# A four-layer attention kernel: the second up half of the gated layer moves to another PSUM bank, and the top-ten layer selects its rows in column strips

## The reference

```python
# layer 1
scores = einsum('bnd,d->bn', base_hidden, score_w[0]) + score_b[0]
_, topk_idx = top_k(scores, 10)
sparse_hidden = take_along_axis(base_hidden, topk_idx[:, :, None], axis=1)
...
return base_hidden.at[arange(B)[:, None], topk_idx].set(attn_out)
# layer 2, end
x = silu(x @ Wgate) * (x @ Wup) @ Wdown
return residual + x
```

## Time and profile before

| | |
|---|---|
| runs | 1354.81, 1357.92, 1359.65 us (median 1357.92) |
| the profiled execution | 1358.02 us, its span 1356.2 us |
| mean granted TensorE clock | 0.943 of full |
| busy: TensorE, VectorE, ScalarE, GpSimd | 90%, 54%, 45%, 32% |
| instructions | 36206 |
| top-ten layer | about 655 to 785 us of the span |
| grouped layer | about 785 to 1210 us, 16 slots and an end |

### The profile page before, as it was taken

The page is one execution under the profiler, slowest core; times in us unless marked ns, Lnnn a source line. Parts: engine busy times, 40 slices in busy tenths (PEclk is TensorE's granted clock), DMA queues, the critical chain, the costliest instruction groups (busy, mean ns, idle before and its releaser), DMA issues.

```text
span 1356.2 us, 36206 instructions
## 1 busy us (share of the span) xinstructions
PE 1219.7 (90%) x14778; PEld 1028.2 (76%) x14778; DVE 728.2 (54%) x1656; ACT 610.4 (45%) x1464; POOL 428.3 (32%) x545
## 2 busy tenths in 40 slices
PE   4899999977899999999778869999999999998986
PEld 2566666655599999999567759889889888876665
DVE  5688787667322000000466457657656657636776
ACT  2455555422444544545222235445445445535542
POOL 3224446153323222226200134424424423332200
PEclk9999999876899999999866879999999999999998
DMA  9000000000489999999510010100100100000000
GB/s 313 2 2 2 2 2 18 9 17 25 136 287 327 338 354 361 352 354 314 179 52 2 2 41 22 40 22 21 41 22 21 41 22 21 21 2 1 18 17 33
DMA packets 91572, 130.73 MB, mean 96 GB/s; under 512 B 13392, under 2 KB 74064, under 8 KB 91280
## 3 DMA queue, kind: packets, MB, share of 16 engines
q1 hardware_dynamic: 85360, 117.11, 26.0%
q0 software_dynamic: 4768, 10.26, 2.1%
q10 hardware_dynamic: 1280, 1.04, 0.2%
HBM read 116.82 MB, written 11.57 MB: 95 GB/s over the span
## 4 chain that ended last, share of the span: by engine, by line
PE 76%; DVE 11%; issue 4%; ACT 3%; DMA 3%; POOL 2%; SPq 1%; another core or an unknown queue 1%; ACTq 0%; DVEq 0%; POOLq 0%
PE scores L1776 9%; PE bank L1786 9%; PE scores L1470 8%; PE bank L2326 8%; PE bank L491 5%; PE bank L1470 4%; PE scores L508 4%; DVE reg L880 3%; PE scores L518 3%; PE bank L540 3%; PE scores L2316 3%; PE scores L2302 3%; PE bank L500 3%; PE bank L529 2%; PE scores L1978 2%
## 5 line engine op out<-in xcount | busy, mean ns | idle before, releaser
L1821 ACT ACTIVATE w_ca<-scores,fc1b 128x128 f32<-128x128 f32 x312 | 114.1, 367 | 139.3 <-PE scores L1776 117.2
L1776 PEld LDWEIGHTS scores<-reg 128*128 128x128 f32 x1248 | 145.2, 192 | 7.0 <-issue 2.5
L1776 PE MATMUL scores<-reg 128*128 128x128 f32 x1248 | 146.3, 275 | 3.8 <-DMA reg<-in_fc 1.2
L880 DVE TENSOR_REDUCE reg<-scores 128x8 f32<-128x1024 f32 x96 | 113.0, 1220 | 64.2 <-PE scores L508 55.6
L2396 ACT ACTIVATE reg<-reg,mx 128x128 f32<-128x128 f32 x256 | 99.3, 389 | 106.8 <-DVE mx L2547 106.8
L1855 DVE TENSOR_TENSOR reg<-bank,reg 128x256 f32<-128x256 f32 x39 | 16.6, 425 | 240.9 <-PE bank L1786 225.5
L1786 PE MATMUL bank<-reg,w_ca 128*128 128x256 f32 x624 | 141.1, 379 | 0.3 <-DVE small L1846 0.3
L1786 PEld LDWEIGHTS bank<-reg,w_ca 128*128 128x128 f32 x624 | 115.6, 190 | 14.5 <-DVE small L1846 0.3
L1470 PEld LDWEIGHTS scores<-reg 128*128 128x128 f32 x1024 | 116.8, 192 | 1.9 <-ACT reg L2404 1.1
L1470 PE MATMUL scores<-reg 128*128 128x128 f32 x1024 | 117.0, 275 | 0.5 <-ACT reg L2404 0.5
L2326 PE MATMUL bank<-reg,w_ca 128*128 128x256 f32 x496 | 115.1, 385 | 0.0
(11 more groups left out here) (305 smaller groups left out, 2375.2 us busy)
## 6 DMA issues: line engine op xcount, KB each, us to landing
reg<-in_fc SPq DMA_DIRECT2D x78, 1024.0 KB
w_sa<-grouped_values SPq DMA_DIRECT2D x64, 128.0 KB, 2.6
reg<-expert_out SPq DMA_DIRECT2D x16, 256.0 KB, 3.5
xres<-in_x SPq DMA_DIRECT2D x4, 512.0 KB, 11.4
ctxr<-in_ctx SPq DMA_DIRECT2D x1, 2048.0 KB, 15.3
w_l<-in_w_l SPq DMA_DIRECT2D x2, 1024.0 KB, 13.0
routed_rows<-reg SPq DMA_DIRECT2D x8, 256.0 KB
grouped_values<-reg SPq DMA_DIRECT2D x16, 128.0 KB, 1.7
```

What stands on the lines that cost most here:

```text
L880: ins = nc.vector.tensor_reduce(mxpad.rearrange("p (c n d) -> p n c d", c=C, d=DH)[:, 4 * half:4 * half + 4, :, 0], scores4[:, 2 * half:2 ...
L1776: ins = nc.tensor.matmul(S[n % 4][:, 0:P], up_w8[j % 2][:, c, f * P:(f + 1) * P], xbT[:, j % 2, c, :], start=(c == 0), stop=(c == C - 1))
L1821: nc.scalar.activation(h1[:, j % 2, f, :], S[n % 4][:, 0:P], ACT.Gelu, bias=fc1b[:, bass.ds(e * FC + f, 1)]).then_inc(M["fc1_free"], 1)
```

## The change

**Grouped layer.** The job u1 gets home "c" (bank 7, where the second query half qb lives) in slots t < B - 1, that is for batches 0 to 13. In slots 15 and 16 it stays in bank 0. The order of instructions is the same on every engine.

**Top-ten layer.** `chosen_rows` takes the selector of a batch (128 x 32) as the stationary side and the batch's 256 columns of xres as the moving side, and writes to the 32 partitions of the bank that belong to the batch: job "xr". The rows come out unturned. ScalarE copies them, with the turned selector, to chosen_T. A new TensorE step, `turn_chosen`, turns the two 128x128 halves into a new job "xg", and a new ScalarE step, `turned_copy`, writes them over the unturned ones. For groups 1 to 3 `turn_chosen` stands behind the value products of the group before, ahead of the queries; `turned_copy` stands ahead of `even_heads`. For group 0 both follow at once.

```diff
--- before.py
+++ after.py
@@
         tok_turned = junk[:, 0:4, :].rearrange("p k n -> p (k n)")
 
         KV = ["hc0", "hc1", "k0", "k1", "v0", "v1"]
-        in_turn = [("bias", 0)] + [(n, 2) for n in KV] + [("row", 0), ("xg", 0), ("q", 0)]
+        in_turn = [("bias", 0)] + [(n, 2) for n in KV] + [("row", 0), ("xr", 0), ("xg", 0), ("q", 0)]
         for g in range(G):
             if g + 1 < G:
-                in_turn += [("row", g + 1), ("xg", g + 1)]
+                in_turn += [("row", g + 1), ("xr", g + 1)]
             in_turn += {1: [("hc0", 3), ("hc1", 3)], 2: [("v0", 3), ("v1", 3)]}.get(g, [])
             if g + 1 < G:
-                in_turn += [("q", g + 1)]
+                in_turn += [("xg", g + 1), ("q", g + 1)]
             in_turn += {1: [("k0", 3), ("k1", 3)]}.get(g, [])
             if g + 1 == G:
                 in_turn += [("at", 0), ("at", 1), ("qa", 0), ("qb", 0), ("kv", 0)]
@@
         IN_TOP_TEN = [("at", 0), ("at", 1), ("qa", 0), ("qb", 0), ("kv", 0)]
         for t in range(-2, B + 1):
             for name, ahead, home in SLOT_JOBS:
+                if name == "u1" and t < B - 1:
+                    home = "c"
                 if 0 <= t + ahead < B and (name, t + ahead) not in IN_TOP_TEN:
                     job_at[name, t + ahead] = (home, n_jobs[home])
                     n_jobs[home] += 1
@@
                 ins.then_inc(tok_done(("row", g)), 1)
 
             def chosen_rows(g):
+                bank = tok_claim(pe, ("xr", g))
+                pe.wait_ge(M["tok_gat_ok"], g + 1)
+                for j in range(GB):
+                    nc.tensor.matmul(bank[mine(j), 0:D], gat[:, j, :], xres[:, g * GB + j, :], start=True, stop=True)
+                nc.tensor.transpose(bank[:, D:D + P], gat[:, :, :].rearrange("p j r -> p (j r)"), ident[:])\
+                    .then_inc(tok_done(("xr", g)), 1)
+
+            def turn_chosen(g):
                 bank = tok_claim(pe, ("xg", g))
-                pe.wait_ge(M["tok_gat_ok"], g + 1)
+                tok_await_moved(pe, ("xr", g))
                 for c in range(C):
-                    for j in range(GB):
-                        nc.tensor.matmul(bank[:, c * P + j * R:c * P + (j + 1) * R], xres[:, g * GB + j, c * P:(c + 1) * P],
-                                         gat[:, j, :], start=True, stop=True)
-                nc.tensor.transpose(bank[:, C * P:C * P + P], gat[:, :, :].rearrange("p j r -> p (j r)"), ident[:])\
-                    .then_inc(tok_done(("xg", g)), 1)
+                    ins = nc.tensor.transpose(bank[:, c * P:(c + 1) * P], chosen_T[:, g % 2, c * P:(c + 1) * P], ident[:])
+                ins.then_inc(tok_done(("xg", g)), 1)
 
             def queries(g):
                 bank = tok_claim(pe, ("q", g))
@@
             values(1, 2)
             score_rows(0)
             chosen_rows(0)
+            turn_chosen(0)
             queries(0)
             scores(0)
             for g in range(G):
@@
                 if g + 1 == G:
                     l2_keys_values(pe, 0)
                 if g + 1 < G:
+                    turn_chosen(g + 1)
                     queries(g + 1)
                 if g == 1:
                     keys(0, 3)
@@
                     .then_inc(tok_moved((f"v{v}", g)), 1)
 
             def chosen_copy(g):
-                bank = tok_await(act, ("xg", g))
+                bank = tok_await(act, ("xr", g))
                 if g >= 2:
                     act.wait_ge(M["tok_put_full"], g - 1)
-                nc.scalar.activation(chosen_T[:, g % 2, :], bank[:, 0:3 * P], ACT.Copy).then_inc(tok_moved(("xg", g)), 1)
+                nc.scalar.activation(chosen_T[:, g % 2, :], bank[:, 0:3 * P], ACT.Copy).then_inc(tok_moved(("xr", g)), 1)
+
+            def turned_copy(g):
+                bank = tok_await(act, ("xg", g))
+                nc.scalar.activation(chosen_T[:, g % 2, 0:D], bank[:, 0:D], ACT.Copy).then_inc(tok_moved(("xg", g)), 1)
 
             def queries(g):
                 bank = tok_await(act, ("q", g))
@@
             values(0, 2)
             values(1, 2)
             chosen_copy(0)
+            turned_copy(0)
             queries(0)
             for g in range(G):
                 if g + 1 == G:
@@
                 if g == 2:
                     values(0, 3)
                     values(1, 3)
+                if g + 1 < G:
+                    turned_copy(g + 1)
                 even_heads(g)
                 if g + 1 < G:
                     queries(g + 1)
@@
                 dve.sem_inc(tok_moved(("row", g)), 1)
                 link(nc.vector.tensor_tensor(place[:, own], n_above[:, own], n_tied[:, own], ALU.add))
                 if g > 0:
-                    tok_await(dve, ("xg", g - 1))
+                    tok_await(dve, ("xr", g - 1))
                 for j in range(GB):
                     ins = nc.vector.tensor_scalar(gat[:, j, :], ranks, place[:, g * GB + j:g * GB + j + 1], None, ALU.is_equal)
                 ins.then_inc(M["tok_gat_ok"], 1)
```

## The result

| | before | changed |
|---|---|---|
| runs | 1354.81 to 1362.88 us, median 1358.42 (5) | 1328.60 to 1342.55 us, median 1339.60 (5) |
| the profiled execution | 1358.02, span 1356.2 | 1328.60, span 1326.8 |
| instructions | 36206 | 36166 |

The ratio is 0.9853, with a 95% interval of 0.981 to 0.9896: 14 to 26 us less, 20 at the middle. Predicted were 18.9 us and 1339.

What follows compares the result with a forecast made beforehand. The chain of waits, three quarters of it TensorE, was taken to bound the kernel. -14.0 (grouped layer) - 4.9 (top-ten layer) = -18.9 us, from 1358.0 to 1339 us; own range 1334 to 1344, for 8 in 10 1333 to 1348.

Steps and rivals of the forecast that it cites:

- Edit 1: Grouped layer: second up half to bank 7 removes 14 holes ahead of the value products; -14.0 us, bounds 11.6 to 14.4.
- The selection: Top-ten layer: eight selector instructions in four overlapping strips take 1.1 us instead of 3.6, 2.5 us off each.
- The end "no overlap": Top-ten selection, other end of the estimate: strips run serially, 8 x 0.46 = 3.65 us, no gain at all.
- rival 1: Top-ten selections: strips don't overlap and stay at 3.65 us; -10.6 us in all, 1347 us; chance 0.07.
- The turns, group by group: Top-ten layer: turning chosen rows between value products and queries costs 1.2 us at half clock, 0.9 at full.
- Edit 2: Top-ten layer: selection in strips, then turning the chosen rows; -4.9 us together, bounds -5 - 5 and +3.4.
- Rival 2: Top-ten layer, group 3: TensorE loses its full clock, +11 us, so -8 in all, 1350 us; chance 0.06.
- Rival 3: Grouped layer: another wait fills the hole, or u1 stays in bank 0's order; -4.9 alone, 1353 us; chance 0.03.
- rival 4: Top-ten layer and first grouped slot: TensorE's clock lost throughout, kernel slower; 1369 us with 30 lost; chance 0.02.

Runs made afterwards that it cites:

- edit 1 alone: Second up half of batches 0 to 13 in bank 7, top-ten layer as in the kernel before: median 1342.83 us, ratio 0.991 to the kernel before.
- Edit 2 alone: Changed kernel with the second up half back in bank 0, keeping the strip selection and turns: median 1351.97 us, ratio 0.9969 to the kernel before.
- the turns ahead: Changed kernel with the chosen rows turned ahead of the value products in groups 1 and 2: median 1336.33 us, ratio 0.9853 to the kernel before.
- all three fillings: Changed kernel plus unread matmuls behind the scores of groups 1 to 3, ahead of turned scores of groups 0 to 2, behind group 0's scores: 1327.96 us, ratio 0.9785.

## Why the prediction was right

**Edit 1: right, and a little more than its upper bound.** The cause was read as the wait for bank 0 behind VectorE's last gate multiplication; the run with the wait restored shows it. Taken were 14.0 us, bounds 11.6 to 14.4. Measured: slots of 24.47 instead of 25.46 or more. From the products of slot 0 to those of slot 14, a stretch with all 14 seams, at a granted clock of 0.99 in both, the kernel before took 358.77 us (801.93 to 1160.70) and the changed one 343.60 (786.04 to 1129.64): 15.2 less. The whole grouped layer got 13.4 shorter, since the half-rate piece in slot 15 took 1.6 more. The 15.0 with edit 1 alone hold the same piece and a first slot at a higher clock (23.64 us; 25.39 in the changed kernel), and the two nearly cancel. A slot gains 0.99 us where the hole was 0.94, so the seam itself got 0.05 us tighter; that the slot's other seams leave no idle time was right, and the upper bound, made of the holes alone, was 0.8 us too low. The new wait for the query bank cost nothing, with 3.7 us to spare as worked out.

**The selection: right.** 1.08 us measured, 1.1 taken from the strips of the last layer, doubled twice. The end "no overlap" is what the one-strip run shows, 3.62. The changed kernel shows weight loads of a median 138 ns for the eight instructions, and the eight still pass in 1.08 us. The rule of the Trainium skill (page "TensorE: Matmul & The Clock Gate", Part 3, "The mechanism"), that loads overlap running matmuls only across row groups, doesn't hold for these column strips. It doesn't hold within one strip either: there the loads had a median of 177 ns, and the eight passed in 3.62 us, which is 8 x 0.45, the matmuls' own time at half rate, with none for a load between them. The prediction took only a part of that section, which also lets a load run ahead when it goes to a background weight buffer; so the page as a whole speaks less clearly against the overlap than rival 1 made it.

**The turns, group by group.** Time from one fixed place to the next, before and changed:

| | taken | measured | |
|---|---|---|---|
| opening, selection to queries | -1.3 | -1.16 | 4.54, now 3.38 |
| group 0, turned scores to next scores | -0.5 | -0.61 | 16.52, now 15.91; products -1.7 as taken |
| group 1, the same | -0.7 | -1.84 | 20.02, now 18.18 |
| group 2, the same | -2.4 | -2.27 | 20.77, now 18.50 |
| between the groups | 0 | +0.6 | clock |

Group 1 is the one that is off. Its products gained 2.05 (taken 1.95), so the working held so far. Then the changed kernel's products took 1.30 us and its queries 1.13, the full rate, where the kernel before still ran at half rate through the products (1.94). That is the clock, and between groups 0 and 1 it went the other way: scores 2.59 instead of 1.90, put-back 1.05 instead of 0.71. The sum, -5.25, is near the -4.9 taken partly since the two cancel, which is luck. So it is with the whole: the stages of the two profiles differ by -13.4 and -5.25, together -18.7, beside the -18.9 forecast, though the seams alone gave 15.2 where 14.0 were taken. Edit 2 alone measured 4.2 us by its ratio, between 1.2 and 7.2.

**The rivals.** Rival 1 (no overlap) fell to the profile and the one-strip run. Rival 2 (group 3 loses its clock) did happen, in three profiled executions: edit 2 alone, the wait back and the turns ahead, where the group took 24.6 us each time, 4.9 more than the 19.7 of the changed kernel's first profile. Priced at 11, it cost half. The code of this layer is the same in both profiles of the changed kernel and in the one with the wait back, and its group 3 took 19.7, 21.2 and 24.6 us; so it varies from execution to execution. The prediction treated it as a property of the kernel with a chance; a part of it belonged in the range. Whether edit 2 makes it more frequent isn't shown: the two profiles without edit 2 (the kernel before and edit 1 alone) have 19.8 and 20.2 us there, and two are too few. Rival 3 (another wait fills the hole) fell: VectorE's last turn ends 1.8 us ahead. Of rival 4 (the clock lost throughout) nothing was seen.

Within the intervals the edits add up: ratios of 0.991 and 0.9969 alone multiply to 0.9879; both together gave 0.9853 and 0.9877.

## What to carry to other kernels

Where TensorE has one regular hole per round and the wait view says only "issue", look at what the other engines finish just ahead of the hole's end, and at the banks that the next instructions claim; a job can be moved to another bank at no cost when that bank's last reader is done some us earlier. A selection with a narrow selector belongs on the stationary side with its outputs in different strips: four strips took 1.08 us where one took 3.62. The rows then come out unturned, and turning them cost 1.0 to 1.3 us each time, from the turns to the queries. Before a few us are fought for in a stage with short waits, read its granted clock: here filling the waits of TensorE with matmuls whose results nobody reads was worth 8 to 11 us, about twice as much as the selection (4.2 us by its ratio).

## What was not expected of the hardware

Unread matmuls in TensorE's waits took 8 to 11 us off the time (the median went from 1339.25 to 1329.53, 1330.84 and 1327.96, with ranges that don't touch the changed kernel's). The turned scores, 128 instructions, took 7.05 us behind waits of 2.5 us and 1.1 to 1.75 us, and 3.77 or 3.78 us in the profile with all three fillings; the layer's granted clock rose from 0.72 to 0.85. The version with all three fillings beats both kernels: 0.9785 of the kernel before.

The clock also goes with the spread between executions. Of 25 runs of the kernel before on one chip, the nine with a mean granted clock of 0.945 or more took 1349.59 to 1355.67 us, the six at 0.940 or less 1358.81 to 1360.69. The same code ahead of the top-ten layer took 674.23 us in one profile and 663.48 in another, and the top-ten layer of the changed kernel between 107.15 us at a granted clock of 0.71 and 114.00 at 0.65 (the run with the wait back), while slots 2 to 13 of the changed kernel agreed within 0.02 us from one profile to the other. A single profiled execution can therefore show a change of 5 us only stage by stage, and never by its span.
